# Four gather buffers, weights in PSUM, and corners weighted by ScalarE in one phase of a four-layer image kernel

## The reference, cut to what matters

```
layer 0: linear attention in chunks of 1024 pixels, then a group norm
layer 1: a 3x3 conv gives an offset per channel and pixel; x is sampled there
         (bilinear, clamped: "deform"), then a 3x3 conv
layer 2: a 3x3 convolution (by FFT in the reference)
layer 3: sim = cosine similarity of each pixel with its 8 neighbours
         om = conv3x3(concat(x, sim))          # 27 channels: 18 offsets, 9 masks
         for each of 9 taps k and each pixel: the 4 corners around the offset position,
           val[c,k] = mask * (g00*w00 + g01*w01 + g10*w10 + g11*w11)
         out = einsum(val, weight) + bias
```

## Time and profile before

| | us |
|---|---|
| median of 3 runs | 10819.47 |
| lowest and highest | 10759.67, 10827.76 |
| the profiled execution, its time | 10817.34 |
| its span | 10815.4 |

### The profile page before, as it was taken

One profiled execution on the slowest core, in us unless ns is written; L12 is line 12 of the kernel. 1 busy time (PEld: TensorE's weight loads), 2 busy tenths in 40 slices (PEclk: granted clock), 3 DMA queues, 4 the chain that ended last, 5 costly groups with the idle time before them and its releaser, 6 DMA issues. The chain is left out here.

```text
span 10815.4 us, 89281 instructions
## 1 busy us (share of the span) xinstructions
PE 6241.5 (58%) x24786; PEld 3752.8 (35%) x24786; DVE 6512.2 (60%) x7322; ACT 2175.6 (20%) x3684; POOL 6260.0 (58%) x5206
## 2 busy tenths in 40 slices
PE   4544895667765774567765775567775762121121
PEld 3322433445543233345543233345542221111111
DVE  5799326679964445689954446689954443333333
ACT  2332221223211311222211311223302310000000
POOL 0000005767766356767767357777766357777777
PEclk8776897778887886678887886788887875555555
DMA  2000013322232323322232323322233323333333
GB/s 63 18 0 17 28 40 103 95 90 78 77 98 86 105 79 111 95 87 77 79 96 87 105 81 108 92 91 77 77 97 94 95 87 97 98 96 97 97 97 90
DMA packets 447223, 888.33 MB, mean 82 GB/s; under 512 B 119848, under 2 KB 269694, under 8 KB 444028
## 3 DMA queue, kind: packets, MB, share of 16 engines
q0 software_dynamic: 248832, 679.81, 21.3%
q1 hardware_dynamic: 194812, 131.49, 4.3%
q10 hardware_dynamic: 3456, 75.50, 1.7%
HBM read 764.88 MB, written 121.53 MB: 82 GB/s over the span
## 5 line engine op out<-in xcount | busy, mean ns | idle before, releaser
L611 POOL DMA_INDIRECT gathered_corners<-gather_table,metas x5184 | 6251.7, 1206 | 4531.2 <-issue 3121.3
L670 DVE TENSOR_TENSOR gathered_corners<-gathered_corners,metas 128x2304 f32<-128x2304 f32 x432 | 1105.4, 2559 | 1755.5 <-DMA gathered_corners<-gather_table,metas 1631.1
L1241 PE MATMUL ps<-ident,sampled 128*128 128x128 f32 (+1 forms) x2160 | 490.6, 381 | 2496.2 <-DVE sampled L675 2439.0
L1039 ACT COPY sampled_by_channel<-ps 128x512 f32<-128x512 f32 x576 | 336.8, 585 | 4829.6 <-PE ps L1241 2959.8
L1241 PEld LDWEIGHTS ps<-ident,sampled 128*128 128x128 f32 (+1 forms) x2160 | 326.8, 184 | 2710.9 <-issue 2604.7
L1312 PE MATMUL ps<-region,woff 128*128 (+1 forms) x3456 | 1182.4, 499 | 23.6 <-ACT region L1024 23.6
L1238 PE MATMUL ps<-ident,weighted_corners 128*128 128x128 f32 (+1 forms) x5760 | 850.8, 316 | 253.9 <-DVE weighted_corners L668 252.0
L1238 PEld LDWEIGHTS ps<-ident,weighted_corners 128*128 128x128 f32 (+1 forms) x5760 | 806.2, 218 | 339.1 <-issue 208.1
L839 DVE TENSOR_TENSOR work<-work 128x768 f32<-128x768 f32 x960 | 889.9, 955 | 17.8 <-ACT work L1102 11.1
L1312 PEld LDWEIGHTS ps<-region,woff 128*128 128x128 f32 x3456 | 654.7, 192 | 499.7 <-issue 49.4
L1225 PE MATMUL ps<-sampled_by_channel,w 128*64 128x256 f32 x2880 | 737.9, 475 | 97.0 <-issue 50.3
(11 more groups left out here) (207 smaller groups left out, 7303.8 us busy)
## 6 DMA issues: line engine op xcount, KB each, us to landing
gathered_corners<-gather_table,metas POOLq DMA_INDIRECT x5184
x_after_layer<-region ACTq DMA_DIRECT2D x8, 4608.0 KB, 12.3
gather_table<-tabst SPq DMA_DIRECT2D x192, 192.0 KB, 2.5
region<-in_x_dram ACTq DMA_DIRECT2D x12, 1536.0 KB
region<-x_after_layer ACTq DMA_DIRECT2D x4, 4608.0 KB, 15.1
res<-x_after_layer SPq DMA_DIRECT2D x144, 128.0 KB
out_dram<-ob SPq DMA_DIRECT2D x144, 128.0 KB
indices_and_weights<-region SPq DMA_DIRECT2D x24, 540.0 KB, 4.5
```

What stands on the lines that cost most here:

```text
L611: pool.indirect_dma_start(out=G[:, s % NG, k, :], out_offset=None, in_=table, in_offset=bass.IndirectOffsetOnAxis(ap=idx[:, s * KK + k:s * ...
L670: ch.own(ch.after().tensor_tensor(Gs, Gs, w.unsqueeze(2).to_broadcast([128, 4 * KK, C]), ALU.mult))
L1241: mm = pe.transpose(out_m, V[:, s % 2, 128 * m:min(128 * m + 128, KK * C)], ident[:, :])
```

## The change

Buffers. `NG` is 4, one for each step of a group. The sum is left in place: `sampled(s)` is now the first 576 floats of `G[:, s]`, so `V` and `W` are gone, PE transposes out of the gather buffer, and GpSimd waits for `transposed` of step n - 4 instead of `weighted` of step n - 2.

Weights. In `weigh`, step 0 copies the group's 144 weights from `metas` to PSUM bank 4, and the multiplies of all four steps read them there. What used bank 4 before moves: the attention matrices to bank 7, the transposed maximum to bank 3, with a new semaphore `max_read` before PE writes bank 3 again.

Deform. There is no summing on PE any more. ScalarE multiplies: for each of 9 x 4 corners of a step one activation of 128 x 64 elements in place, with the weight as a per-partition `scale` from a copy `wact`; it then increments `weighed`, and VectorE does the two adds (`add_corners`). The places move: steps 0 to 3 behind rounds 1 to 4, and `finish` of a group at place 0 of the next tile. ScalarE's `turned` of steps 0, 1, 2 stand two places later, and that of step 3 in front of the next tile.

```diff
-NG = 2
+NG = 4
+WTS = STEPS * 4 * KK
-PLACES = {0: ((), (), (), (), (), ()),
-          1: (((0, 0),), (), ((0, 1),), ((0, 2),), ((0, 3),), ((0, None),))}
+PLACES = ((), (), (0,), (1,), (2,), (3,))
...
-        V = sb("sampled", [128, 2, KK * C])
-        W = sb("weighted_corners", [128, 4, KK * C])
+        wact = sb("weights_of_group", [128, WTS])
...
+        def sampled(s):
+            return G[:, s].rearrange("p k x -> p (k x)")[:, 0:KK * C]
...
-                            pool.wait_ge(weighted, j * (2 * STEPS) + (e * STEPS + s + 1 - NG + CREDIT))
+                            pool.wait_ge(transposed, j * (2 * STEPS) + (e * STEPS + s + 1 - NG + CREDIT))
...
+                def weigh(g, slot, s):
+                    Gs = G[:, s].rearrange("p k (q c) -> p (k q) c", c=C)
+                    v.wait_ge(gathered[s], (g + 1) * (KK * 16))
+                    if s == 0:
+                        in_sbuf = metas[:].rearrange("p e m -> p (e m)")
+                        ch.own(ch.after().tensor_copy(ps[:, 4, 0:WTS], in_sbuf[:, bass.ds(slot * META + STEPS * KK, WTS)]))
+                    w = ps[:, 4, s * 4 * KK:(s + 1) * 4 * KK]
+                    ch.own(ch.after().tensor_tensor(Gs, Gs, w.unsqueeze(2).to_broadcast([128, 4 * KK, C]), ALU.mult))
+
+                def add_corners(g, s):
+                    Gq = G[:, s]
+                    ch.own(ch.after().tensor_tensor(Gq[:, :, 0:2 * C], Gq[:, :, 0:2 * C], Gq[:, :, 2 * C:4 * C], ALU.add))
+                    ch.named(ch.after().tensor_tensor(sampled(s).rearrange("p (k c) -> p k c", c=C), Gq[:, :, 0:C], Gq[:, :, C:2 * C], ALU.add),
+                             weighted, g * STEPS + (s + 1 + CREDIT))
...
                         def place(at):
-                            for gi, s in PLACES[tiles_groups[e]][at]:
-                                steps_of(j + G_TAPS[e], (j + G_TAPS[e]) % 2, (s,))
+                            if sample and at == 0:
+                                finish(j + (G_TAPS[e] - 1))
+                            for s in PLACES[at] if sample else ():
+                                v.wait_ge(weighed, t * STEPS + (s + 1))
+                                add_corners(j + G_TAPS[e], s)
...
-                        ch.own(ch.after().tensor_reduce(mxrow, ps[0:1, 4, 0:128], AX.X, ALU.max))
+                        ch.named(ch.after().tensor_reduce(mxrow, ps[0:1, 3, 0:128], AX.X, ALU.max), max_read, t + 1)
...
+                        def weigh(s):
+                            if not sample:
+                                return
+                            act.wait_ge(gathered[s], (j + (G_TAPS[e] + 1)) * (KK * 16))
+                            if s == 0:
+                                weights = metas[:].rearrange("p e m -> p (e m)")[:, bass.ds((j + G_TAPS[e]) % 2 * META + STEPS * KK, WTS)]
+                                ch.after()
+                                ch.own(nc.scalar.copy(wact[:, :], weights))
+                                ch.after()
+                            for k in range(KK):
+                                for q in range(4):
+                                    corner = G[:, s, k, C * q:C * q + C]
+                                    n = (s * KK + k) * 4 + q
+                                    ins = nc.scalar.activation(corner, corner, ACT.Identity, bias=zero[:, 0:1], scale=wact[:, n:n + 1])
+                            ins.then_inc(weighed, 1)
+
+                        steps_of(j + (G_TAPS[e] - 1), (3,))
                         act.wait_ge(clipped, t + 1)
...
                         for ia in range(2 * R + 1):
                             if ia >= 2:
-                                place(ia - 2)
+                                weigh(ia - 2)
+                            if ia >= 3:
+                                steps_of(j + G_TAPS[e], (ia - 3,))
                             act.wait_ge(hat_used, t * 5 + (ia + 1))
...
-                        for at in (3, 4, 5):
-                            place(at)
+                        weigh(3)
+                        steps_of(j + G_TAPS[e], (2,))
...
-                        if sum_on_pe:
-                            for q in range(4):
-                                mm = pe.matmul(out_m, W[:, q, 128 * m:min(128 * m + 128, KK * C)], ident[:, :],
-                                               start=q == 0, stop=q == 3)
-                        else:
-                            mm = pe.transpose(out_m, V[:, s % 2, 128 * m:min(128 * m + 128, KK * C)], ident[:, :])
+                        mm = pe.transpose(out_m, sampled(s)[:, 128 * m:min(128 * m + 128, KK * C)], ident[:, :])
```

109 lines of the change are left out of this document (46 added, 63 removed).

## The result

The changed kernel takes 11309.27 us (median of 4; 11295.26 to 11345.21) against 10821.09 us for before (10759.67 to 10827.76): a ratio of 1.0469, 95% interval 1.0423 to 1.0516. The forecast was 10200, faster. The profiled execution has a span of 11319.2 us and a granted clock of 0.722. That is half of the result. In the last experiments before ran at 10483 to 10485 us, and there the same changed kernel took 10114, a ratio of 0.9647. What follows is about what lies between the two.

The account below looks back on a forecast made before the run. GpSimd's gathers, with VectorE in their way, were taken to bound the last stage, and VectorE deform. Three stages of -154 us (-462) and the last stage's -155 made -617: 10817 - 617 = 10200 us, range 10000 to 10500.

Parts of the forecast that it names:

- Weights in PSUM free the gathers: Gathers under the multiply L670 take 0.95 us instead of 2.56 once one operand comes from PSUM, saving 1.61 a step.
- the ring of deform: Deform tile: ScalarE's stream and VectorE's adds wait on each other in a loop, 74.3 us against 65.7, +104 a stage.
- c: Deform: ScalarE's time for each of 144 small activations a tile, taken as 0.325 us, bounds 0.20 and 0.419.
- The sign that ScalarE's busy time grows: Profile check for the whole kernel: ScalarE busy from 2176 by 5184 x 0.419 to some 4350 us.
- Last stage, attention, convolutions, offsets: Phases set by the gathers' rate: last stage -155 us; attention -55, convolutions -94, offsets -86 a stage.
- a term of 1.1 us a group: First step of a group: weights copy and `finish`, waiting for a 5.2 us projection, shift L672 later, costing 1.1.
- without that cover `finish` would cost up to its 6.6: Deform: `finish` at place 0 comes over 8 us after the adds, covering about 6.6 us of transposes and projection.
- What is late next is the gather under L672: Once L670 no longer delays gathers, the one under L672, with two SBUF inputs, costs 0.55 us a step.
- C: Rival, slower than before: each of deform's 144 activations also pays for fetch and start; 11107 at 0.50 us, chance 0.04.
- The gaps of convolutions (60.9 a group) and offsets (64.6): Before's convolutions and offset phase run slower than the gathers' rate because two buffers pass stalls between VectorE and GpSimd.
- 104 forecast: Deform loss for each stage: 12 tiles, each 8.6 us longer, +104 us.

Follow-up runs that it names:

- the last experiments: Final two blocks of runs, with before at 10483 to 10485 us; the changed kernel, unchanged, took 10114.2 us there, 0.9647 of before.
- the two kernels made for the last two questions: Changed kernel with an extra PE semaphore raised without a matmul, 10127.9 us; changed kernel with half the projection before the fourth transposes, 10146.0 us.
- The version with the split but no breaks: Changed kernel with VectorE weighing the second and fourth step of each deform tile, ScalarE the first and third: 9945.4 us, 0.9485 of before.
- `e7_memsets`: Changed kernel with four waited GpSimd memsets of 128x16 behind each step's nine gathers: 10671.4 us, 0.9916 of before.
- `e11_memset_and_split`: Changed kernel with one waited memset behind each step, and VectorE weighing each deform tile's second and fourth step: 10659.2 us, 0.9956 of before.

## Why the prediction was wrong, point by point

- **Weights in PSUM free the gathers:** right. A gather under the multiply takes 0.95 us (9709.22 in after, under L665 from 9708.29), the mean fell to 1066 ns (forecast: about 1030). On the inference in SBUF — State Buffer, section Who interferes with whom, of the Trainium skill, that tensor_tensor doesn't starve descriptor generation, the trace disagrees again: its other sentence, on two SBUF inputs, is the one that the runs bear out (gathers take 1158 ns on average with the weights read from SBUF outside deform, 1066 with PSUM weights).
- **ScalarE and the ring of deform:** right, 74.2 against 74.3. c was taken as 0.325 us; 36 activations take 12.04 us, 0.334 each. The sign that ScalarE's busy time grows "from 2176 by 5184 x 0.419 to some 4350 us" was worked out wrongly: it takes 0.419 for each and forgets the overlap that c has. With c it would be 2176 + 5184 x 0.325 = 3860; measured are 3888.
- **Last stage, attention, convolutions, offsets:** the forecast's periods are those of the kernel where PE's increments aren't held: 47.9 for 46.7, 48.3 for 45.6 (VectorE's own chain, which I had put at 45.6 too, sets it: VectorE stands only 14 us before the multiply in these eight chunks, as the four full buffers carry it through), 393 for 376, 305 for 307. The forecast of 10200 is 86 us above the 10114 measured there. In part that is luck: it was reckoned from 10817, and before itself ran at 10483 beside the 10114. The forecast gain is 617, the measured one 369.
- **The step that failed** is the price of waits for PE. `finish` "waits for a projection of 5.2 us" and stood in a term of 1.1 us a group; "without that cover `finish` would cost up to its 6.6"; and "What is late next is the gather under L672". What was late next, in the runs that the result comes from, was the increment of `proj_done`, with waits of up to 48.9 us, then `transposed` and the convolutions' semaphores. It isn't a mis-sized term but a missing one. No rival had it: C had a slower kernel through ScalarE's start cost, and that cost isn't there.
- **A second error, in reading before.** The gaps of convolutions (60.9 a group) and offsets (64.6) I put down to two buffers. Part of them may have been held increments, 1335 us of idle time in all engines; in the last runs before is 337 us faster (10821 to 10484). There is no trace of before from those runs, so by how much its phases shrank isn't shown.

The balance: where increments are held the change costs 488 us: 65 in the last stage (1943.4 - 1878.6 between its first and last gather) and about 141 in each of three stages, of which the tiles of deform have 116 in stage 2 (838.6 - 723.0), 104 forecast. Where they aren't held, the tiles take 74.2 us all the same, and the change as a whole brings 369 us, the buffers and PSUM weights outweighing deform; how the 369 are made up isn't shown, for want of a trace of before there.

## What to carry to other kernels

Before you make a producer's stream denser, look at what in it lets others through: here a stall that the change removed had also been the break in which another engine's semaphores got out. Read the waits that the profile can't assign as a measurement, not as a remainder: their sum (1335, 3203, 10 us) told the two conditions apart at once. Look too whether the trace is whole: where increments are missing from it, as here, the recording may be part of what you measure. Let ScalarE and VectorE take a shared job in turns, not in blocks; and measure a change of a few per cent beside its base more than once, since the condition that decides it may not be the kernel's. Here the same change is 1.0469 in one and 0.9647 in the other.

## What the runs showed of the hardware

- With indirect gathers 0.30 us apart, and in one of two conditions, an increment of PE reached VectorE 37 us after the end that PE's row gives (waits of up to 48.9 us), 4.0 to 9.2 us after the last gather; ScalarE and GpSimd saw it too (714 and 228 us). Increments of VectorE and ScalarE didn't show this: 33 and 20 are late in both conditions, of PE's matmuls 471 and 33. A gap of 1.89 us every 12 us let nearly all of those of `finish` through, one of 1.1 us a part.
- The profile can't tell whether the matmuls end late or only their increments. The Trainium skill, Perfetto Trace Analysis, section Per-engine timelines, says that TensorE's end is estimated from the instruction's size, and that its semaphore is raised when PSUM has acknowledged the last bytes. The held time would lie behind that estimated end; no run here shows where.
- Whether increments are held is a condition outside the kernel: one chip showed both (before at 10766 and at 10485 us). What sets it, whether the recording of the semaphores has a part in it, whether only increments of matmuls are held, and whether a burst of PE's work matters, stays open; the two kernels made for the last two questions ran where nothing was held.
- The version with the split but no breaks, 0.9485 of before, wasn't run where increments are held; by the 176 us expected of the split (169 measured, 10114 to 9945) it would be near 11130 there, an estimate. Two versions with breaks that were run there come out under before, both by less than 1% (`e7_memsets` 0.9916, `e11_memset_and_split` 0.9956).
